# Block 0 of a language-model tower: the Hadamard steps across four 128-column chunks on TensorE instead of VectorE

## The reference

```python
h = 1
while h < n:                      # n = 512
    x = x.reshape(-1, n // (2 * h), 2, h)
    a, b = (x[:, :, 0, :], x[:, :, 1, :])
    x = jnp.stack([a + b, a - b], axis=2).reshape(-1, n)
    h *= 2
# ffn: x = fwht(x * SU_ug) / SCALE, then up, gate, silu(gate) * up,
# fwht over 2048, and W_down
```

## Time and profile before

| | |
|---|---|
| median of 3 runs | 1306.49 us (1306.09 to 1312.7) |
| the profiled execution, its own time | 1306.45 us |
| its span, first to last instruction | 1304.6 us |
| mean granted clock of PE | 0.979 of full speed |
| busy: PE, DVE, ACT, POOL | 1226.0, 660.7, 436.0, 574.7 us |
| the tail of block 0 in the span | from about 98 to 129.6 us |

### The profile page before, as it was taken

One profiled execution on the slowest core, in us unless ns is written; L12 is line 12 of the kernel. 1 busy time (PEld: TensorE's weight loads), 2 busy tenths in 40 slices (PEclk: granted clock), 3 DMA queues, 4 the chain that ended last, 5 costly groups with the idle time before them and its releaser, 6 DMA issues.

```text
span 1304.6 us, 18006 instructions
## 1 busy us (share of the span) xinstructions
PE 1226.0 (94%) x6718; PEld 584.9 (45%) x6718; DVE 660.7 (51%) x1252; ACT 436.0 (33%) x828; POOL 574.7 (44%) x492
## 2 busy tenths in 40 slices
PE   7865879889999999999999999999999999999998
PEld 4552334334444444444444444444444444444444
DVE  2589599555564545544644545454554454451110
ACT  4874665521243023411432134302341143212210
POOL 1462487411575237531764166523753176311210
PEclk9987889999999999999999999999999999999999
DMA  9810144543452344333443345234433343120000
GB/s 322 309 33 1 33 73 87 107 97 65 113 106 59 95 104 106 65 81 90 109 93 73 87 107 106 51 96 104 106 65 81 93 109 82 33 73 9 1 1 32
DMA packets 230904, 112.86 MB, mean 87 GB/s; under 512 B 209400, under 2 KB 210736, under 8 KB 230320
## 3 DMA queue, kind: packets, MB, share of 16 engines
q1 hardware_dynamic: 219632, 77.52, 26.6%
q0 software_dynamic: 10240, 33.56, 9.3%
q10 hardware_dynamic: 960, 0.75, 0.2%
HBM read 52.82 MB, written 9.70 MB: 48 GB/s over the span
## 4 chain that ended last, share of the span: by engine, by line
PE 77%; DVE 9%; POOL 5%; ACT 4%; issue 3%; DMA 2%; SPq 0%; ACTq 0%; DVEq 0%; POOLq 0%
PE bank L1434 24%; PE bank L1435 24%; PE bank L1436 24%; DMA att<-ids_b 1%; POOL p L529 1%; PE bank L1610 1%; DVE wd L689 1%; POOL h_row L556 1%; POOL hid L580 1%; DVE a L1036 1%; PE bank L1429 1%; DVE h L677 1%; ACT sg L1147 1%; PE bank L1660 1%; PE bank L1499 1%
## 5 line engine op out<-in xcount | busy, mean ns | idle before, releaser
L1434 PE MATMUL bank<-xT,wgu 128*128 128x512 f16 x1024 | 391.4, 382 | 4.7 <-DVE a L1036 2.8
L1435 PE MATMUL bank<-xT,wgu 128*128 128x512 f16 x1024 | 391.3, 382 | 0.0
L1436 PE MATMUL bank<-xT,wgu 128*128 128x512 f16 x1024 | 391.0, 382 | 0.0
L580 POOL TENSOR_TENSOR hid<-a,hid 128x512 f16<-128x512 f32 x128 | 174.4, 1362 | 171.5 <-ACT hid L1150 171.3
L1036 DVE SCALAR_TENSOR_TENSOR a<-bank,kap,sg 128x512 f32<-128x512 f32 x128 | 96.0, 750 | 299.5 <-PE bank L1436 225.3
L1434 PE MATMUL bank<-wd,hid 128*128 128x512 f16 x512 | 195.2, 381 | 0.0
L1436 PE MATMUL bank<-wd,hid 128*128 128x512 f16 x512 | 195.1, 381 | 0.0
L1435 PE MATMUL bank<-wd,hid 128*128 128x512 f16 x512 | 195.1, 381 | 0.0
L1434 PEld LDWEIGHTS bank<-xT,wgu 128*128 128x128 f16 x1024 | 101.1, 99 | 125.1 <-issue 6.3
L1436 PEld LDWEIGHTS bank<-xT,wgu 128*128 128x128 f16 x1024 | 100.8, 98 | 123.0 <-issue 3.8
L1435 PEld LDWEIGHTS bank<-xT,wgu 128*128 128x128 f16 x1024 | 100.7, 98 | 118.7 <-issue 2.8
(11 more groups left out here) (223 smaller groups left out, 1470.0 us busy)
## 6 DMA issues: line engine op xcount, KB each, us to landing
out<-a SPq DMA_DIRECT2D x24, 256.0 KB
wgu<-in_L_ffn_W_gate SPq DMA_DIRECT2D x4, 1024.0 KB, 14.8
wgu<-in_L_ffn_W_up SPq DMA_DIRECT2D x4, 1024.0 KB, 15.0
wd<-in_L_ffn_W_down SPq DMA_DIRECT2D x4, 1024.0 KB, 15.8
out<-h_row SPq DMA_DIRECT2D x8, 256.0 KB
hid<-att_table,ids_p POOLq DMA_INDIRECT x72, 3.6
xT<-in_L_tok_proj_weight SPq DMA_DIRECT2D x1, 1024.0 KB, 8.6
p<-in_L_attn_Wq SPq DMA_DIRECT2D x1, 1024.0 KB, 12.0
```

Source lines behind the costliest of these rows:

```text
L580: nc.gpsimd.tensor_tensor(hid[:, 1, s, :], a32[:, :], hid[:, 0, s, :], ALU.subtract)\
L1434: mm(dst, w[0], v[0], start=first, stop=False)
L1435: mm(dst, w[0], v[1], start=False, stop=False)
L1436: return mm(dst, w[1], v[0], start=False, stop=final)
```

## The change

For block 0 alone, the two butterflies are left out: DVE's `row_norm` returns behind L988. ACT's `x_high` waits for the scaled row (`xs_done`) in place of `xm_done`. PE's `x_mix` sums the four chunks itself: for each of the four output chunks `row` it runs 4 (input chunks k) x 2 (halves l) matmuls of 128 columns with the Hadamard matrix or its negative as weights, 32 in place of 2. The negative matrix `hada_minus` is made once by DVE in slot 2 of block 0's attention. The other blocks keep their butterflies, and their semaphore counts shift by four.

```diff
+        hada_minus = late[:, 1024:1088].bitcast(F16)
@@ DVE, row_norm
                 nc.vector.scalar_tensor_tensor(wide[:, :], row, mv[:, 0:1], su_b[:, :], ALU.subtract, ALU.mult)\
                     .then_inc(S["xs_done"], 1)
+                if first(n):
+                    return
                 dve.wait_ge(S["xs_done"], i + 1)
                 butterfly(halves(x_mid, P), halves(wide[:, :], P)).then_inc(S["xa_done"], 1)
-                dve.wait_ge(S["xa_done"], i + 1)
+                dve.wait_ge(S["xa_done"], i - 3)
                 butterfly(halves(wide[:, :], 2 * P), halves(x_mid, 2 * P)).then_inc(S["xm_done"], 1)
@@ DVE, slot s of block 0's attention
                 if s == 2:
                     val_low()
+                    dve.wait_ge(S["t_ready"], 16)
+                    nc.vector.tensor_scalar(hada_minus, hada16[:, :], -1.0, None, ALU.mult).then_inc(S["minus_ready"], 1)
@@ ACT, x_high
-                act.wait_ge(S["xm_done"], 4 * n + m + 1)
+                if first(n):
+                    act.wait_ge(S["xs_done"], m + 1)
+                else:
+                    act.wait_ge(S["xm_done"], 4 * (n - 1) + m + 1)
@@ PE, x_mix
+                if first(n):
+                    pe.wait_ge(S["minus_ready"], 1)
+                    for row in range(DC):
+                        for k in range(DC):
+                            sign = hada_minus if bin(row & k).count("1") % 2 else hada16[:, :]
+                            for l in range(2):
+                                c = (DC * l + k) * P
+                                last = mm(PICK[1][:, row * P:row * P + P], sign, xn16[:, c:c + P],
+                                          start=k == 0 and l == 0, stop=k == DC - 1 and l == 1)
+                    last.then_inc(S["xhada_ready"], 1)
+                    return
                 mm(PICK[1][:, :], hada16[:, :], xn16[:, 0:512], start=True, stop=False)
                 mm(PICK[1][:, :], hada16[:, :], xn16[:, 512:1024], start=False, stop=True).then_inc(S["xhada_ready"], 1)
```

More of the change, by code:

```diff
@@ L244, in tower @@
         emb_ss nw_turned et_copied blk_set gb_land gm_ready qk_sq t_ready t_copied vt_ready vt_copied proj_ready tok_ready x1_ready qk_ready v_ready
-        prm_ready prm_copied hada16_ready
+        prm_ready prm_copied hada16_ready minus_ready
         feat_ready score_ready a_sq a_hi a_lo v_hi v_lo wo_hi wo_lo wo_scale wo_sum
```

## The result

| | before | after |
|---|---|---|
| median of 20 runs | 1306.61 us (1305.85 to 1316.09) | 1311.68 us (1306.3 to 1318.21) |
| profiled execution, its own time | 1306.45 | 1307.57 |
| its span, mean granted clock | 1304.6, 0.979 | 1305.8, 0.982 |
| first `wo_rows` matmul to first gate matmul ("the tail") | 98.38 to 129.59: 31.2 us | 98.96 to 131.85: 32.9 us |

The ratio after / before is 1.0028, 95% interval 1.0014 to 1.0041: slower by 3.7 us (1.8 to 5.4), less than the 0.5% bound of the prediction. The distance of the medians is 5.1 us. The 20 runs after lie around 1311.7, and the profiled one, at 1307.6, is the second fastest of them. That will matter.

A forecast was written before the change was run, and what follows sets the result against it. The tail of block 0 was taken as bound by DVE, then by a ring of PE and ACT; +0.7 at full clock, +1.5 for one low-clock pass and -0.7 saved made +1.5 us on 1306.5: 1308.0 us, range 1303.8 to 1312.0.

The forecast's parts named there:

- 0.5% bound of the prediction: Whole kernel: about 0.5%, 6.5 us, is what a measurement can tell from no change; chance of staying within 0.89.
- The removal, -5.9 us of DVE on the path: Block 0's tail: four passes of butterflies, 1.47 us each, leave DVE's path; 5.9 us is the most to gain.
- The price of `x_mix`: PE in block 0's tail: 32 matmuls of 128 columns take 2.0 us at 2.4 GHz, 3.6 at 1.2 GHz.
- Rival 4: Weight loads show in x_mix, 2.9 us even at full clock: +3.6 us on the forecast, 1311.6; chance 0.05.
- `x_flip(0)` and `x_mix(0)` 1.5 us earlier: First pass of the tail on PE: x_flip(0) moves from 109.94 to 108.5, x_mix(0) from 112.99 to 111.5.
- The ring: PE and ACT in the tail: x_mix, xT_high, two square sums, x_copied, next x_mix; 5.13 us a pass at full clock.
- Rival 3: DVE's saving comes through whole, if ACT were not held to its written order: -5.9 us, 1300.6; chance 0.06.
- The full-clock sum, +0.7: End of the tail: with the clock at full level throughout, first gate matmul at 130.3 instead of 129.59, +0.7 us.
- The clock, +1.5 and -0.7: PE in the tail: one pass at 1.2 GHz costs 1.5 us; half of the first gate matmuls' 1.4 us is saved.
- rival 2: Lower clock from the second pass on, three passes at 1.2 GHz: +5.2 us, 1311.7; chance 0.10.
- The shift passes through one to one.: Behind the tail: engines start by semaphores from the first gate matmuls' results, so the tail's shift carries through unchanged.
- a difference behind 150 us: Sign of a wrong forecast: a difference that arises behind 150 us of the span, which no term has.

The follow-up runs named there:

- e2: Kernel before with block 0's butterflies left out but x_mix kept at 2 matmuls of 512 columns: tail 27.4 us, median 1304.88 us, ratio 0.9983.
- e3: Changed kernel with DVE's butterflies kept, x_high waiting for them, and x_mix of 32 matmuls: tail 34.3 us, median 1311.81 us, ratio 1.0037.
- e4: Changed kernel with ACT's two square sums of each pass placed ahead of xT_high: tail 30.3 us, median 1307.88 us, ratio 1.0009.
- e9: Changed kernel with DVE's row_norm(m) placed ahead of xT_low(m-2), ACT's order untouched: tail 34.4 us, median 1311.93 us, ratio 1.0026.
- e5: Changed kernel with 8 matmuls without a use behind each x_mix and x_flip: tail 31.3 us, median 1304.55 us, ratio 0.9989.
- e1: Changed kernel run again with no edit, for a second profile: tail 35.5 us, median 1310.74 us, ratio 1.0034.
- e10: e4 with DVE's row_norm also placed ahead of xT_low: tail 28.0 us, median 1303.82 us, ratio 0.9975.
- e11: e10 with 4 matmuls without a use behind each x_mix and x_flip: tail 28.0 us, median 1303.69 us, ratio 0.9978.

## Why the prediction came out as it did

- **The removal, -5.9 us of DVE on the path.** The butterflies are gone from DVE's path. That all 5.9 us could arrive is not shown: the most that did is 3.8 us of the tail, in e2, where `x_mix` stays short.
- **The price of `x_mix`.** Right: 1.95 to 1.97 us (2.0 forecast) and 3.2 to 3.6 at 1.2 GHz (3.6). The 32 start 56 ns apart. The Trainium skill's 81 ns (TensorE: Matmul & The Clock Gate, "Back-to-back issue gap") is not what the runs show for this stream; its other figure there for 128 columns, about 56 ns for the isolated gap, is. Rival 4 falls.
- **`x_flip(0)` and `x_mix(0)` 1.5 us earlier.** Right: 108.91 and 111.96, less the 0.58 us by which this execution's tail began later, are 108.3 and 111.4 (108.5 and 111.5 forecast).
- **The ring.** Right in its members, 4.92 us for 5.13: `x_copied` follows the start of `xT_high` by 1.86 us, not 2.01. e3, e4 and e9 each single it out. Rival 3 falls.
- **The full-clock sum, +0.7.** e5 has it almost pure: tail 31.3 against 31.2, so +0.1, and 0.15 of that tail is the filling; the three passes at 0.2 less make most of the difference. So at full clock the change neither lengthens nor shortens the tail.
- **The clock, +1.5 and -0.7.** The mechanism holds, the size was taken too small for the median. In the profiled execution it came out close: `x_mix(2)` took 2.5 us and `x_mix(3)` 3.2, together 1.8 over the full clock, the tail was 1.7 us longer, and the whole 1.4 us of the gate matmuls back (from the first gate matmul to the next matmul after it that waits for a sum over the partitions, 151.07 - 129.59 = 21.5 before and 151.93 - 131.85 = 20.1 after). The median is where rival 2 had its time, 1311.7, to which I had given 0.10: three passes low. e1 and e9, the two other profiles of this pattern, have three passes low or partly low. That the typical execution is like them is argued from two profiles and from e5's gain, not shown. The term that was mis-sized is "one pass at 1.2 GHz" (+1.5).
- **"The shift passes through one to one."** Not quite: behind the tail the clock is lost once more in some executions (264 to 276 us), 1.7 us in e1. No term had that. The forecast named a difference behind 150 us as a sign that it is wrong, and here is one, though it is a matter of the clock and differs between executions of the same kernel.
- **The total.** 1308.0 was forecast, range 1303.8 to 1312.0. The median is 1311.68, 0.3 us inside the upper end; by the ratio it is 3.7 us over before, where the forecast said 1.5. That it stays within 0.5% held. That the profiled execution came out at +1.1, close to +1.5, is partly luck: +0.6 arose ahead of the tail, where no term stood, the full-clock sum was 0.6 too high, and the clock cost and gave back more than was forecast (+1.8 and -1.4 for +1.5 and -0.7).

What stays open: why filling gives the kernel before 2.9 us although its tail keeps its length, and why typical runs after the change, if they are like e1, have more low passes than the first profile. The runs show only that equal work can go either way, and that the profiles with a full clock from 105 to 140 us are those with the shortest stretch behind the first gate matmul (1172.8 to 1173.5 us, against 1173.9 to 1179.9).

## What to carry to other kernels

When work is taken from the engine that has no gaps, follow the chain of the next engine's written order before counting the gain: here an idle PE stood in a ring with two square sums that had nothing to do with it. The 1.6 us of longer matmuls per pass used up the 1.5 us of removed additions even at full clock, and the lower clock made a loss of it. Moving such a bystander into a wait that its engine has anyway (e4), and then cutting the next ring (e10), turned a loss of 4 us into a probable gain of about 3 (the tail is 3.2 us shorter; the interval of the time just touches no change) with the same instructions. And where PE works in bursts with idles of 2.5 us, one profile shows one outcome of the clock: take a second before sizing that term.

## What the runs showed of the hardware

- The granted clock of a short burst is not settled by the kernel's instructions and their times in the tail: at the second `x_mix`, reached after 2.52 us of idle at 116.87 and 116.93 us of the span and behind the same instructions, one execution had 2.4 GHz and the other 1.2. With idles of 1.1 to 1.2 us ahead of each `x_mix` (e10) or below 0.3 us (e11) all four ran at 2.4 GHz, in one profile each.
- Filling idle stretches with matmuls without a use lowered the median by 6.2 us in the changed kernel (e5 against e1, on two chips on which the kernel before had medians of 1307.26 and 1307.27), by 2.7 us in e4, and by 2.9 us in the kernel before, with no other edit; in e10, where the idles are short already, by nothing (1303.82 and 1303.69).
